# Slice-attention temperatures on 128 partitions, expert weights loaded at the second convolution, sigmoid attention on row and column tiles

## What is computed

```python
def reference(x, ...):
...
    t = _to_tokens(x)
    t = t + _L2_attn_ref(_ln_t(t), ...)
    t = t + _L2_ffn_ref(_ln_t(t), ...)
    t = t + _L3_attn_ref(_ln_t(t), L3_attn_q_weight)
    t = t + _L3_ffn_ref(_ln_t(t), ...)
    x = _from_tokens(t, x)

def _L2_attn_ref(x, W_x, b_x, W_slice, b_slice, W_temp, b_temp, W_out, b_out):
...
    x_proj = (x @ W_x.T + b_x).reshape(B, N, H, D).transpose(0, 2, 1, 3)
    adaptive_temp = BASE_TEMP + jnp.clip(x_proj @ W_temp.T + b_temp, -0.4, 0.4)
    log_neg_log_eps = jnp.log(-jnp.log(jnp.float32(EPSILON)))
    slice_logits = x_proj @ W_slice.T + b_slice - log_neg_log_eps
    slice_weights = jax.nn.softmax(slice_logits / adaptive_temp, axis=2)
...

def _L3_attn_ref(input, q_weight):
...
    query = jnp.einsum('bnd,de->bne', input, q_weight)
    att = jax.nn.sigmoid(jnp.einsum('bnd,bmd->bnm', query, input))
    value = jnp.einsum('bnm,bmd->bnd', att, input)
    return value
```

## Time and profile before

| | |
|---|---|
| median of 3 runs | 1390.83 us (1389.59 to 1392.49) |
| the profiled execution | 1390.77 us, span 1389.0 us |
| PE busy | 1070.2 us (77% of the span) |
| DVE busy | 872.3 us (63%) |
| ACT busy | 525.4 us (38%) |
| POOL busy | 265.8 us (19%) |
| mean granted TensorE clock | 0.774 of full speed |
| slice attention stage | about 337.4 to 472.8 us of the span |
| sigmoid attention stage | about 951.7 to 1020.4 us |

### The profile page before, as it was taken

The page is one execution under the profiler, slowest core; times in us unless marked ns, Lnnn a source line. Parts: engine busy times, 40 slices in busy tenths (PEclk is TensorE's granted clock), DMA queues, the critical chain, the costliest instruction groups (busy, mean ns, idle before and its releaser), DMA issues. The chain is left out here.

```text
span 1389.0 us, 27111 instructions
## 1 busy us (share of the span) xinstructions
PE 1070.2 (77%) x9518; PEld 620.5 (45%) x9518; DVE 872.3 (63%) x2483; ACT 525.4 (38%) x1346; POOL 265.8 (19%) x375
## 2 busy tenths in 40 slices
PE   6678877677899756666666666668973899999996
PEld 2366652252555434544545445445743333333332
DVE  6585745745777455555555555554246588888885
ACT  3443433353443322222222222234440555444552
POOL 3404012200000000000000000000000155555555
PEclk9888997878999855555555555558995999999998
DMA  8000000000000000000000000000000675555550
GB/s 286 1 1 1 1 2 1 0 1 1 1 0 1 1 1 0 0 0 0 0 0 0 0 0 0 0 0 1 0 0 0 128 159 122 122 125 129 120 123 25
DMA packets 23059, 46.99 MB, mean 34 GB/s; under 512 B 1616, under 2 KB 5840, under 8 KB 22608
## 3 DMA queue, kind: packets, MB, share of 16 engines
q1 hardware_dynamic: 22992, 46.10, 14.1%
HBM read 43.47 MB, written 2.62 MB: 33 GB/s over the span
## 5 line engine op out<-in xcount | busy, mean ns | idle before, releaser
L1606 PE MATMUL wide<-ls_h,ls_v 128*128 128x16 f16 x2304 | 104.8, 177 | 144.8 <-DVE ls_h L1705 141.5
L2110 ACT ACTIVATE ex_gated<-wide,unscale 128x1024 f32<-128x1024 f32 x128 | 142.1, 1113 | 139.2 <-PE wide L2076 139.1
L2126 DVE TENSOR_TENSOR ex_hid<-wide,ex_gated 128x1024 f32<-128x1024 f32 x128 | 155.9, 1223 | 45.4 <-ACT ex_gated L2110 40.9
L1606 PEld LDWEIGHTS wide<-ls_h,ls_v 128*128 128x128 bf16 x2304 | 81.6, 106 | 213.8 <-DVE ls_h L1705 213.8
L2052 POOL TENSOR_TENSOR ex_acc<-ex_part,ex_acc 128x512 f32<-128x512 f32 x120 | 152.3, 1269 | 95.0 <-DVE ex_part L2142 80.8
L1695 DVE TENSOR_TENSOR_SCAN ls_cells<-ls_terms 128x48 f32<-128x48 f32 x256 | 73.6, 288 | 124.1 <-ACT ls_terms L1630 124.1
L1630 ACT ACTIVATE ls_terms<-wide 128x32 f32<-128x32 f32 x256 | 54.5, 213 | 229.5 <-PE wide L1611 229.5
L2088 PE MATMUL wide<-ex_hid,w 128*64 128x512 f32 x512 | 116.7, 598 | 0.0
L2076 PE MATMUL wide<-xh,wh 64*128 64x512 f16 x512 | 98.9, 382 | 5.3 <-PEq L81 3.4
L2076 PE MATMUL wide<-xh,wl 64*128 64x512 f16 x512 | 98.1, 379 | 0.0
L2076 PE MATMUL wide<-xl,wh 64*128 64x512 f16 x512 | 97.9, 378 | 0.0
(11 more groups left out here) (365 smaller groups left out, 1992.5 us busy)
## 6 DMA issues: line engine op xcount, KB each, us to landing
ex_d<-route SPq DMA_DIRECT2D x64, 512.0 KB, 8.0
par_attn<-in_attn SPq DMA_DIRECT2D x1, 2704.0 KB, 13.9
par_rest<-in_rest SPq DMA_DIRECT2D x1, 2139.0 KB, 18.4
L_xin<-in_x SPq DMA_DIRECT2D x8, 256.0 KB, 6.1
w<-in_w SPq DMA_DIRECT2D x1, 2048.0 KB, 22.8
out<-ex_acc SPq DMA_DIRECT2D x16, 128.0 KB, 4.6
w<-in_w SPq DMA_DIRECT2D x1, 512.0 KB, 23.6
route<-ro_dt SPq DMA_DIRECT2D x8, 64.0 KB, 1.7
```

What stands on the lines that cost most here:

```text
L1606: pe.matmul(ig[:, g, :] if g < 2 else o, vp[part][:, g, :], h1[:], start=False, stop=False, skip_group_check=True)
L2110: act.activation(gated[:, n % 2, :], pair_of_up(n // GS, 2 * (n % GS))[:], ACT.Silu, scale=m.unscale[:, 0:1]).then_inc(s["gated_ready"], 1)
L2126: dve.tensor_tensor(hid[:, n % (2 * GS), :], pair_of_up(n // GS, 2 * (n % GS) + 1)[:], gated[:, n % 2, :], ALU.mult).then_inc(s["hid_ready ...
```

## The change

Three edits are made together.

1. The temperatures are worked on all 128 partitions: `temperatures()` issues eight matmuls, each 32 output rows by 128 columns, the four column quarters q going to the four groups of 32 output partitions. DVE's three operations are then 128 partitions x 128 elements. `spread(h)` takes four matmuls of 128 columns with four selecting matrices in place of one of 512 columns. `par_rest` grows by 800 columns.
2. `w12` and `w3` are loaded by SP at the start of the second convolution stage and are allocated there, in place of the start of the program.
3. In the sigmoid attention the zeroed `sg_qz` becomes `sg_qs` with one copy; scores of the two halves contract 64 rows each and are issued alternately for halves 0 and 1; the values alternate in the same way between output partitions 0 to 63 and 64 to 127. `n` becomes `2b + h`.

```diff
                     sp.dma_start(m.chunk[name][:], m.dram[name]).then_inc(s, 16)
+        else:
+            @block.sync
+            def _(sp):
                 sp.dma_start(m.w12[:], m.dram["w12"]).then_inc(m.moe_landed, 16)
                 sp.dma_start(m.w3[:], m.dram["w3"]).then_inc(m.moe_landed, 16)
...
                     for h in range(2):
-                        mm = pe.matmul(TM[0:R, :], p["temp_rows"][:, h * R:(h + 1) * R], xps[:, h, :],
-                                       start=(h == 0), stop=(h == 1))
+                        for q in range(4):
+                            mm = pe.matmul(TM[32 * q:32 * (q + 1), 0:P], p["temp_rows"][:, 32 * h:32 * (h + 1)],
+                                           xps[:, h, q * P:(q + 1) * P], start=(h == 0), stop=(h == 1),
+                                           skip_group_check=True)
...
-                    pe.matmul(TM[:], p["temp_spread"][:, h * P:(h + 1) * P], temp[:], start=True, stop=True)\
-                      .then_inc(s["spread_done"], 1)
+                    for q in range(4):
+                        mm = pe.matmul(TM[:, q * P:(q + 1) * P], p["temp_spread"][:, (4 * h + q) * P:(4 * h + q + 1) * P],
+                                       temp[:], start=True, stop=True)
+                    mm.then_inc(s["spread_done"], 1)
...
-                    dve.tensor_scalar(temp[0:R, :], TM[0:R, :], p["b_temp"][0:R, 0:1], 0.4, ALU.add, ALU.min)\
+                    dve.tensor_scalar(temp[:], TM[:, 0:P], p["b_temp"][:, 0:1], 0.4, ALU.add, ALU.min)\
...
-                    dve.reciprocal(temp[0:R, :], temp[0:R, :]).then_inc(s["inv_temp"], 1)
+                    dve.reciprocal(temp[:], temp[:]).then_inc(s["inv_temp"], 1)
...
-                def scores(n):
-                    h, b = n // 2, n % 2
-                    pe.wait_ge(s["att_ready"], 4 * t + n + 1)
+                def scores(b):
+                    pe.wait_ge(s["att_ready"], 4 * t + 2 * b + 2)
                     for q in range(2):
-                        mm = pe.matmul(bank[SB[n]][:, q * HW:(q + 1) * HW],
-                                       x[:, k, (2 * b + q) * P:(2 * b + q + 1) * P],
-                                       qz[:, k, h, b * HW:(b + 1) * HW], start=True, stop=True)
-                    mm.then_inc(s["s_done"], 1)
+                        for h in range(2):
+                            r = slice(C * h, C * (h + 1))
+                            mm = pe.matmul(bank[SB[2 * b + h]][:, q * HW:(q + 1) * HW],
+                                           x[r, k, (2 * b + q) * P:(2 * b + q + 1) * P],
+                                           qs[r, k, b * HW:(b + 1) * HW], start=True, stop=True)
+                            if q:
+                                mm.then_inc(s["s_done"], 1)
...
+                def values(b):
+                    pe.wait_ge(s["att_ready"], 4 * t + 2 * b + 6)
                     for q in range(2):
+                        for h in range(2):
+                            mm = pe.matmul(bank[k][C * h:C * (h + 1), b * HW:(b + 1) * HW],
+                                           xt[:, k, (2 * b + q) * P + C * h:(2 * b + q) * P + C * (h + 1)],
+                                           att[:, 2 * b + h, q * HW:(q + 1) * HW], start=(q == 0), stop=(q == 1),
+                                           skip_group_check=True)
...
-                    for h in range(2):
-                        r = slice(C * h, C * (h + 1))
-                        act.activation(qz[r, 1 - k, h, :], bank[4][r, :], ACT.Copy).then_inc(s["q_ready"], 1)
+                    act.activation(qs[:, 1 - k, :], bank[4][:], ACT.Copy).then_inc(s["q_ready"], 1)
...
-            dve.memset(qz[:], 0.0).then_inc(s["zeroed"], 1)
```

More of the change, by code:

```diff
@@ L55 @@
                  x_weight=1, eps5=1, lstm_half=1, w_x=256, b_x=1, w_slice=128, b_slice=1,
-                 temp_rows=2 * 2 * HEADS, temp_spread=256, b_temp=1,
+                 temp_rows=2 * 32, temp_spread=2 * 4 * 128, b_temp=1,
                  w_out=256, b_out=1, u_i=128, u_g=128, u_o=128, v_i=128, v_g=128, v_o=128,
@@ L1243, in slice_attention_stage @@
         xps = sb("xps", [P, 2, TW])
-        temp = sb("temp", [P, TW])
+        temp = sb("temp", [P, P])
         inv, logit = sb("inv", [P, 2, TW]), sb("logit", [P, 2, TW])
@@ L1741, in sigmoid_attention_stage @@
         x = sb("x", [P, 2, TW])
-        qz = sb("qz", [P, 2, 2, TW])
+        qs = sb("qs", [P, 2, TW])
         xt = sb("xt", [P, 2, TW])
@@ L1745, in sigmoid_attention_stage @@
         wscale = m.wscale
-        names = ("zeroed warm x_ready q_done q_ready xt_done xt_ready s_done att_ready v_done out_ready "
+        names = ("warm x_ready q_done q_ready xt_done xt_ready s_done att_ready v_done out_ready "
                  "wh_ready wl_ready").split()
@@ L1786, in values @@
-                def values(n):
-                    h, b = n // 2, n % 2
-                    pe.wait_ge(s["att_ready"], 4 * t + n + 5)
-                    for q in range(2):
-                        mm = pe.matmul(bank[k][C * h:C * (h + 1), b * HW:(b + 1) * HW],
-                                       xt[:, k, (2 * b + q) * P + C * h:(2 * b + q) * P + C * (h + 1)],
-                                       att[:, n, q * HW:(q + 1) * HW], start=(q == 0), stop=(q == 1))
-                    mm.then_inc(s["v_done"], 1)
+                        for h in range(2):
[5 more added lines that the diff above has]
+                                mm.then_inc(s["s_done"], 1)
@@ new lines, in values @@
+                def values(b):
+                    pe.wait_ge(s["att_ready"], 4 * t + 2 * b + 6)
+                    for q in range(2):
+                        for h in range(2):
[3 more added lines that the diff above has]
+                                           skip_group_check=True)
+                            if q:
+                                mm.then_inc(s["v_done"], 1)
@@ L1795, in step @@
                 if attend:
-                    pe.wait_ge(s["q_ready"], 2 * t + 3)
+                    pe.wait_ge(s["q_ready"], t + 2)
                     scores(0)
-                    scores(1)
                 if prepare:
                     pe.wait_ge(s["x_ready"], u + 1)
-                    pe.wait_ge(s["q_ready"], 2 * u + 1)
+                    pe.wait_ge(s["q_ready"], u + 1)
                     pe.matmul(bank[4][:], p["q_w"], x[:, 1 - k, :], start=True, stop=True).then_inc(s["q_done"], 1)
@@ L1803, in step @@
                 if attend:
-                    scores(2)
-                    scores(3)
+                    scores(1)
                 if prepare:
@@ L1813, in step @@
                     pe.wait_ge(s["out_ready"], t + 1)
-                    for n in range(4):
-                        values(n)
+                    values(0)
+                    values(1)
             run(pe, step)
@@ L1824, in _ @@
             act.wait_ge(s["warm"], 1)
-            act.wait_ge(s["zeroed"], 1)
             def step(t, k, prepare, attend):
@@ L2187, in build @@
         attention_stage(nc, m, m.xa)
+        m.w12 = c.enter_context(nc.sbuf_tensor("w12", [P, 2 * E * HID], F32))
+        m.w3 = c.enter_context(nc.sbuf_tensor("w3", [P, E * C], F32))
         m.stats = c.enter_context(nc.sbuf_tensor("stats", [P, HB, 6], F32))
@@ L2341, in lay_out @@
     mine = [rowed & (np.arange(2 * HEADS)[None, :] // HEADS == h) for h in range(2)]
+    mine = [np.pad(r, ((0, 0), (0, 16))) for r in mine]
     q["temp_rows"] = np.concatenate([np.where(r, np.tile(v["L2_attn_W_temp"].T, (HEADS, 1)), f(0)) for r in mine], 1)
-    q["temp_spread"] = np.concatenate([padded_rows(r.T.astype(f)) for r in mine], 1)
+    chunk = [i[:, None] // 32 == n for n in range(4)]
+    q["temp_spread"] = np.concatenate([np.tile(r.T, (4, 1)) & n for r in mine for n in chunk], 1).astype(f)
     q["b_temp"] = np.repeat(v["L2_attn_b_temp"], P)[:, None]
```

4 lines of the change are left out of this document (1 added, 3 removed).

## The result

| | before | after |
|---|---|---|
| median of the runs compared | 1391.15 us (1389.59 to 1392.49) | 1367.66 us (1366.62 to 1369.42, 4 runs) |
| ratio, 95% interval | | 0.9834 [0.9819, 0.9849] |
| span of the profiled execution | 1389.0 us | 1365.6 us |
| mean granted TensorE clock | 0.774 | 0.772 |

A forecast was written before the change was run, and what follows sets the result against it. PE alone bounds the sigmoid attention; in the slice attention PE's work and bm's chain are within 0.3 us. Gains 16.2 + 5.4 + 0 = 21.6 us off 1390.77 give 1369.2 us, range 1364 to 1377.

The forecast's parts named there:

- A pair of 64-row matmuls in the time of one: Sigmoid attention: full overlap of split matmuls for rows and output columns; scores 2 x 0.86, values 1.73 us per tile.
- A switch costs 0.2: Sigmoid attention: each change between full and split array costs 0.2 us; five per tile, 1.0 us, tile 5.75.
- The first tile gains more: Sigmoid attention's first tile: scores at half clock and 0.60 us less q copy; stage put at -16.2 against 16.0.
- First slice tile, 2.9: Slice attention's first tile: shorter temperature matmuls and no wait for the reciprocal win between 2.3 and 3.7, taken as 2.9 us.
- rule of a fixed rise: Slice attention's first tile: the clock rises at a fixed time, and what is moved ahead of it runs slowly.
- its full 1.2 is won: Slice attention's second tile: it has no output matmuls in it, so PE's whole 1.2 us is won.
- what is late next is bm: Slice attention's steady tiles: bm limits the gain to 0.19 to 0.45 us in six tiles, less 0.06 for spreads; together 1.3.
- TensorE's clock falls in the slice attention: Rival: longer PE waits for bm bring half clock for a few us in each of seven tiles; +8, 1377; chance 0.08.
- The load, 0: Expert weights' load moved later: nothing won or lost, 0 us, bounds 0 and +2.
- ACT did not become the bound: Rival in the sigmoid attention: ACT's chain slips by 0.8 us, each tile takes 0.5 more; +4, 1373; chance 0.12.
- The row pairs did overlap: Rival in the sigmoid attention: row pairs do not overlap, tile 7.5, eight tiles win 2; 1383; chance 0.02.
- the stage at half clock: Slower case: split matmuls use half the array, so the sigmoid attention falls to half clock; 11.4 us tile, 1414; chance 0.02.

The follow-up runs named there:

- experiment 6: Changed kernel with scores(1) issued right behind scores(0) and ACT's q copy behind all four sigmoids: 1365.49 us, ratio 0.9815.
- experiment 7: Changed kernel, but ACT copies q in two halves again: 1370.77 us, ratio 0.9851.
- experiment 5: Changed kernel with scores(1) issued right behind scores(0), ahead of the q matmul, ACT's order unchanged: 1370.93 us, ratio 0.986.
- experiment 10: Changed kernel with DVE's bm before the second scaled logits and maxima, both images' scores together and q copy last: 1354.34 us, ratio 0.9738.
- experiment 4: Changed kernel with value matmuls issued in blocks of one half, each with its own wait, instead of alternating: 1366.51 us, ratio 0.9825.
- bm late: Kernels with DVE's original order, bm behind the scaled logits and maxima of h = 1; the changed kernel so takes 1367.66 us.
- bm ahead: DVE issues bm before the scaled logits and maxima of h = 1; on the changed kernel 1353.89 us, on the kernel before 1385.1 us.

## Why the prediction was right, and where it was not

The total was 1.5 us too high, which is within its own bounds. That is in part luck: the sigmoid attention brought 20.3 us where 14.6 to 18 were allowed, the slice attention 3.2 where 3.5 to 8 were, and the two errors cancel. By its steps:

- **"A pair of 64-row matmuls in the time of one."** Right, for rows and for columns: 1.07 for eight score instructions with a switch in it, 1.88 for sixteen value instructions.
- **"A switch costs 0.2", tile 5.75.** Measured 5.65; with the same 4.75 of work, a switch is 0.18, and experiment 6 gives 0.175. In six steady tiles and the last it makes 0.6 us more gain than forecast.
- **"The first tile gains more."** Right in direction and mis-sized. I counted a shorter group at half clock and 0.60 less of ACT, and put the stage only 0.2 above eight steady tiles. It won 4.15 us to the second tile's scores, 2.1 more than a steady tile. I had priced the removed wait at its own length and had no term for an earlier rise of the clock. It rose at 4.4 instead of 7.8, and experiment 7 shows that the wait of 0.6 us was the cause.
- **The stage behind it.** Not in the sum at all: its first matmuls ran at full clock, 3.87 us instead of 5.37. The sigmoid part so brought 20.3 us, not 16.2. What decides whether these matmuls run at full clock is open; experiments 5 and 10 lost it again.
- **First slice tile, 2.9.** Measured 11.96 - 9.00 = 2.96. Right, but the same rule of a fixed rise served well only here: in both traces the clock rises 3.8 us behind the stage's first transposes.
- **Second slice tile, "its full 1.2 is won".** Wrong: 0.36. I asked only for the output matmuls, and forgot the second use of DVE in that stretch, the tokens' copy behind scaled logits and maxima. It is the same kind of fault in DVE's order as the one that holds bm. This is read from the rows; no run moved the copy.
- **Steady slice tiles, 1.3, "what is late next is bm".** Right: 1.19 from the second copy to the eighth. Per tile, bm to output matmuls fell from 1.03 to 0.75 us, and 0.17 came back in the spreads and in the first instruction behind the wait. The 0.11 net are just under the forecast's least, 0.19 - 0.06; its upper figure, 0.45, was given without a working. The sum still came out because the steps on either side of these four won 0.35 and 0.39, where the wait for bm is 0.55 us and not 0.78.
- **The end of the stage.** Missing in the sum: +1.3, because the clock fell 7 us earlier in the stage. The slice part so brought 3.2 instead of 5.4. The rival "TensorE's clock falls in the slice attention" had the right mechanism in the wrong place: the steady tiles held 1.00 with 12.0 us idle of 90 instead of 7.2, and the fall came in the tail, where it already was.
- **The load, 0.** Right.
- **Rivals.** ACT did not become the bound; the slack was 0.26 where 0.3 was worked out, and experiment 5 shows how little kept it. The Trainium skill, TensorEngine Tiling (Array Packing), PSUM Bottleneck, warns that emptying PSUM may become the limit. In experiment 5 PE did wait 0.30 us a tile for ACT, which empties PSUM, but ACT was busy only 17.1 of 30 us and its order alone removed the wait. The row pairs did overlap, and the stage at half clock did not occur.

So too little was forecast for the sigmoid attention, by 4.1 us, and too much for the slice attention, by 2.2. Of the first about 3.4 (1.9 in the first tile, 1.5 behind the stage) and of the second 1.3 go with TensorE's clock at a stage's first or last microseconds.

## What to carry to other kernels

When a bound shrinks, read the other engine's program order at that place: an item that is covered today (bm here) may stand behind work that nobody waits for. The edit was worth 0.11 us in a tile by itself and 1.16 with the neighbour's order mended, so an edit that wins little should be tried with the next wait taken away before it is dropped. And where PE starts a stage cold, take out short waits in its first microseconds first: the one here, of 0.57 us, cost 1.9 us in its stage. Look behind the stage too, since a shorter stage can lose its gain where the next ones start, as in experiment 10.

## What was not expected of the hardware

- An idle time of PE of 0.57 to 0.67 us, some 3 us into a stage that starts at half clock, goes with a rise of the granted clock 7.3 to 7.8 us behind the first matmul in the five traces that have it; in the seven without it the rise comes at 3.3 to 4.4. Shown both ways, by the change and by experiment 7.
- The clock at the end of the slice attention moves the kernel by 4 to 5.6 us. It fell at a wait of PE of 3.03 us in eight of nine traces with bm late, and stayed at 1.00 in all three with bm ahead, where that wait is 1.50. The ninth is that of experiment 4, where it stayed at 1.00 with the same wait, whose other four times (1365.75 to 1367.96) fit the usual course. So the wait alone does not decide it, and what else does is open; that the ninth trace already differs in the second convolution is the only hint:

```profile
451.17 1.99 PE L1339 MATMUL wide<-sl_ex,sl_bm 128*128 128x256 f32 x8 [3.03 <-DVE sl_bm L1523]
```

- 64-column matmuls for the two column halves overlap almost fully in blocks of four instructions (5.70 us a tile against 5.65).
